# A selective-scan stage with a third buffer for its decay factors, and its gate moved behind the recurrence

## What is computed

```python
xz = x @ in_proj_w.T
u, res = jnp.split(xz, 2, axis=-1)
...
u = jax.nn.silu(conv)
delta = jax.nn.softplus(dt @ dt_proj_w.T + dt_proj_b)
A = -jnp.exp(A_log)
def step(h, t):
    delta_t, B_t, C_t, u_t = t
    dA = jnp.exp(delta_t[..., None] * A)
    h = dA * h + delta_t[..., None] * B_t[:, None, :] * u_t[..., None]
    y = jnp.einsum('bdn,bn->bd', h, C_t)
    return (h, y)
...
y = jnp.swapaxes(ys, 0, 1) + u * D_skip
y = y * jax.nn.silu(res)
return y @ out_proj_w.T
```

## Time and profile before

| | |
|---|---|
| median of three runs | 7221.53 us (7217.19 to 7222.52) |
| profiled execution, its own time | 7217.93 us |
| its span, first to last instruction | 7216.2 us |
| mean granted TensorE clock | 0.875 of full speed |
| DMA | 1297.78 MB |

### The profile page before, as it was taken

How to read it: one execution, slowest core, us unless ns; L and a number is a source line. 1 busy time by engine, 2 the same in 40 slices (tenths; PEclk the granted TensorE clock), 3 DMA queues, 4 the chain that set the end, 5 groups by cost and what they waited for, 6 DMA issues and landing times. The chain is left out here.

```text
span 7216.2 us, 70913 instructions
## 1 busy us (share of the span) xinstructions
PE 5483.0 (76%) x16640; PEld 2999.0 (42%) x16640; DVE 5886.2 (82%) x7907; ACT 3552.3 (49%) x5338; POOL 4301.8 (60%) x2865
## 2 busy tenths in 40 slices
PE   4788778888887888878788888888887888599700
PEld 1344444444444444444444444444444444466400
DVE  5999999999999999989999999999999998211255
ACT  3555555555555555555555555555555554111156
POOL 3666666666666666666666666666666666200176
PEclk8899898889999988898988889989989988699855
DMA  7656556655655555555555555555555555022253
GB/s 262 215 193 197 192 198 200 202 195 195 203 203 188 194 194 191 195 189 194 193 190 189 193 191 200 193 192 189 196 194 184 187 188 194 11 91 87 78 160 94
DMA packets 492087, 1297.78 MB, mean 180 GB/s; under 512 B 59311, under 2 KB 216625, under 8 KB 490561
## 3 DMA queue, kind: packets, MB, share of 16 engines
q1 hardware_dynamic: 440960, 1219.82, 50.7%
q10 hardware_dynamic: 26048, 38.95, 1.6%
q0 software_dynamic: 24576, 33.72, 1.5%
HBM read 1206.19 MB, written 119.54 MB: 184 GB/s over the span
## 5 line engine op out<-in xcount | busy, mean ns | idle before, releaser
L480 POOL TENSOR_TENSOR st<-st,C_rows 128x1024 f32<-128x1024 f32 x1024 | 2470.6, 2415 | 1155.7 <-DVE st L988 1154.3
L787 PE MATMUL y<-st,ident 128*128 128x512 f32 x4096 | 2163.0, 663 | 472.2 <-POOL st L480 426.5
L988 DVE TENSOR_TENSOR_SCAN st<-dA,drive 128x1024 f32<-128x1024 f32 x1024 | 2338.7, 2284 | 177.2 <-ACT dA L642 85.2
L642 ACT ACTIVATE dA<-delta,a_neg 128x511 f32<-128x511 f32 x2048 | 1382.3, 713 | 2155.2 <-DVE st L988 2146.7
L787 PEld LDWEIGHTS y<-st,ident 128*128 128x128 f32 x4096 | 830.3, 212 | 1520.0 <-issue 899.1
L960 DVE TENSOR_TENSOR drive<-du,B_rows 128x1024 f32<-128x1024 f32 x1024 | 1259.5, 1230 | 101.3 <-DVE du L955 18.2
L761 PE MATMUL pre_bank<-e_abs,in_w 128*128 128x512 f32 x1024 | 601.6, 718 | 178.2 <-DVE u L926 161.9
L1388 POOL DMA_INDIRECT rows<-expert_out,idx_c x256 | 266.3, 1040 | 621.5 <-DVE idx_c L1435 551.4
L555 POOL DMA_INDIRECT expert_in<-tb,idx x256 | 259.8, 1015 | 367.0 <-DVE idx_all L1163 306.0
L741 PE MATMUL post_bank<-d_w,gT 128*128 128x256 f32 x2048 | 467.0, 385 | 12.4 <-issue 11.6
L741 PEld LDWEIGHTS post_bank<-d_w,gT 128*128 128x128 f32 x2048 | 394.3, 193 | 119.9 <-issue 67.7
(11 more groups left out here) (190 smaller groups left out, 8027.8 us busy)
## 6 DMA issues: line engine op xcount, KB each, us to landing
B_rows<-bc_rows SPq DMA_DIRECT2D x1024, 512.0 KB
C_rows<-bc_rows SPq DMA_DIRECT2D x1024, 512.0 KB
xin<-in_x SPq DMA_DIRECT2D x32, 512.0 KB, 7.3
expert_in<-gT ACTq DMA_DIRECT2D x8, 2048.0 KB, 27.2
xn_rows<-xin SPq DMA_DIRECT2D x32, 512.0 KB, 6.2
h<-xn_rows SPq DMA_DIRECT2D x32, 512.0 KB, 6.5
x_res<-in_x SPq DMA_DIRECT2D x32, 512.0 KB, 3.6
x_rows<-x_res SPq DMA_DIRECT2D x32, 512.0 KB, 3.2
```

Of the source, the lines that this page charges most:

```text
L480: pool.tensor_tensor(tile[:, :, :], tile[:, :, :], bc[1][k % ROWS[1]][:, :, :], ALU.mult)\
L642: return act.activation(dA[k % 2][:, j, 1:L], delta[par][:, c, 1:L], ACT.Exp, scale=a_neg[:, c, n:n + 1])
L787: last = pe.matmul(Y[:, :], ident[:, :], st[k % RING][:, j, :], start=pair == 0 and j == 0, stop=pair == CU - 1 and j == 1)
L988: dve.tensor_tensor_scan(st[k % RING][:, :, :].rearrange("p a l -> p (a l)"), dA[k % 2][:, :, :].rearrange("p a l -> p (a l)"), DR[:, :, : ...
```

## The change

`dA` gets a third buffer (`AHEAD = 3`), and ScalarE fills `dA` two units ahead of the recurrence in place of one. Units 0 and 1 of a sequence are made at the end of the one before. On VectorE the gate of a finished chunk is called at the end of `recur`, in slot 3k+1, and slot 3k is empty. The counts of `consts` rise by one, for the third buffer's memset.

```diff
+    AHEAD = 3
...
-        dA = [sb(f"dA{i}", [P, 2, L]) for i in range(2)]
+        dA = [sb(f"dA{i}", [P, 2, L]) for i in range(AHEAD)]
...
                 yield 95
-                decay(b, par, 0, 0)
-                decay(b, par, 0, 1).then_inc(scan_exp.did(0), 1)
+                for k in range(AHEAD - 1):
+                    decay(b, par, k, 0)
+                    decay(b, par, k, 1).then_inc(scan_exp.did(k), 1)
...
-                    act.wait_ge(*(scan_h.at(NU - 2 + k, b - 1) if k < 2 else scan_h.at(k - 2, b)))
-                return act.activation(dA[k % 2][:, j, 1:L], delta[par][:, c, 1:L], ACT.Exp,
+                    act.wait_ge(*(scan_h.at((NU - 1 - k) // AHEAD * AHEAD + k, b - 1) if k < AHEAD
+                                  else scan_h.at(k - AHEAD, b)))
+                return act.activation(dA[k % AHEAD][:, j, 1:L], delta[par][:, c, 1:L], ACT.Exp,
                                       scale=a_neg[:, c, n:n + 1])
...
                 def first_half(k):
-                    if k + 1 < NU:
-                        decay(b, par, k + 1, 0)
+                    if k + AHEAD - 1 < NU:
+                        decay(b, par, k + AHEAD - 1, 0)
...
                 def recur(k):
-
                     dve.wait_ge(*scan_exp.at(k, b))
                     dve.wait_ge(*scan_in.at(k, b))
                     dve.wait_ge(*(scan_sum.at(NU - RING + k, b - 1) if k < RING else scan_sum.at(k - RING, b)))
                     dve.tensor_tensor_scan(st[k % RING][:, :, :].rearrange("p a l -> p (a l)"),
-                                           dA[k % 2][:, :, :].rearrange("p a l -> p (a l)"),
+                                           dA[k % AHEAD][:, :, :].rearrange("p a l -> p (a l)"),
                                            DR[:, :, :].rearrange("p a l -> p (a l)"), 0.0,
                                            ALU.mult, ALU.add).then_inc(scan_h.did(k), 1)
-                run_slots(stages, (chunk_done, recur, ahead))
+                    chunk_done(k)
+                run_slots(stages, (nothing, recur, ahead))
```

More of the change, by code:

```diff
@@ L118, in attention_phase @@
     KD, KI, KF, NX, CAP, NSLOT, FAR = (env[k] for k in ("KD", "KI", "KF", "NX", "CAP", "NSLOT", "FAR"))
-    CU, NU, RING, ROWS = (env[k] for k in ("CU", "NU", "RING", "ROWS"))
+    CU, NU, RING, AHEAD, ROWS = (env[k] for k in ("CU", "NU", "RING", "AHEAD", "ROWS"))
     x_v, xn_v, x1_v, xe_dram, bc_dram, xe_zero_v = (
@@ L426, in _ @@
             pool.memset(minus_half[:, :], -0.5).then_inc(consts, 1)
-            for i in range(2):
+            for i in range(AHEAD):
                 pool.memset(dA[i][:, :, 0:1], 0.0).then_inc(consts, 1)
@@ L432, in _ @@
                       allow_small_or_imprecise_dtypes=True).then_inc(consts, 1)
-            pool.wait_ge(consts, 11)
+            pool.wait_ge(consts, 12)
             pool.affine_select(out=ident[:, :], in_=ident[:, :], compare_op=ALU.not_equal, fill=1.0, base=0,
@@ L571, in _ @@
                 act.dma_start(xe_zero_v[a], gT_flat).then_inc(zeroed, 16)
-            act.wait_ge(consts, 13)
+            act.wait_ge(consts, 14)
             act.wait_ge(pre_weights_in, 16 * len(PRE_IN))
@@ L646, in first_half @@
                 def first_half(k):
-                    if k + 1 < NU:
-                        decay(b, par, k + 1, 0)
+                    if k + AHEAD - 1 < NU:
+                        decay(b, par, k + AHEAD - 1, 0)
                 def second_half(k):
-                    if k + 1 < NU:
-                        decay(b, par, k + 1, 1).then_inc(scan_exp.did(k + 1), 1)
+                    if k + AHEAD - 1 < NU:
+                        decay(b, par, k + AHEAD - 1, 1).then_inc(scan_exp.did(k + AHEAD - 1), 1)
                 run_slots(stages, (first_half, second_half, nothing))
@@ L725, in _ @@
                 steps.credit(pe)
-            pe.wait_ge(consts, 13)
+            pe.wait_ge(consts, 14)
             pe.wait_ge(pre_weights_in, 16 * len(PRE_IN))
@@ L898, in _ @@
                 steps.credit(dve)
-            dve.wait_ge(consts, 13)
+            dve.wait_ge(consts, 14)
             dve.wait_ge(pre_weights_in, 16 * len(PRE_IN))
```

## The result

The changed kernel takes 7274.45 us (7269.44 to 7283.53, four runs) against 7221.15 (7217.19 to 7222.52, four runs) for the kernel before in the same comparison: a ratio of 1.0076, 95% interval 1.0059 to 1.0094. It is slower, the direction that had the largest chance, and 4.45 us beyond the upper end of the range. The profiled execution spans 7267.7 us, 51.5 more than before. The lines moved by 1 to 3: L988 is now L990, L787 L790, L741 L744, L1085 L1088, L937 L940, L960 L963, L966 and L969 are L969 and L972, L642 is L645.

A forecast was written before the change was run, and what follows sets the result against it. VectorE (busy 82%) and TensorE (76%) were taken as nearly full. Per sequence −0.7 + 0 + 0.15 + 1.55 = +1.0 us, times 30, less 8 and 4, gave +18: 7235.9 us, with 3.6 for the median 7240; range 7185 to 7270.

The forecast's parts named there:

- Wait at unit 22: VectorE's 1.19 us wait for `dA` goes, L937 then waits 0.4 to 0.5 us: gain 0.7 us a sequence.
- Gate at unit 18: VectorE's mean 1.5 us wait goes, but a longer L937 at unit 20 pays it back: gain 0.
- Gate at unit 10: The gate's 0.55 us wait goes, but VectorE then waits 0.7 us for POOL's `x_res`: loss 0.15 us.
- Gate at unit 26: The gate, which had no wait, comes later: TensorE 2.4 us later, its idle time from 1.03 to 3.4 us.
- Wait at unit 29: The 1.49 us `dA` wait goes, but unit 31's recurrence waits for the ring buffer: all lost again.
- TensorE's clock: Behind unit 26's gap the clock falls, three chances in four; TensorE 3.8 us late, mean loss 1.55 us a sequence.
- The second rival: TensorE keeps its clock behind the gap at unit 26: −0.4 us a sequence, 7197 us; 22%.
- the first number: Unit 31's recurrence starts 1.4 us later; taken as the loss at sequence ends where the loop goes back.
- The sum: +1.0 us in each of 30 sequences, less 8 for slow stretches and 4 for other `dA` waits: +18 us.
- (1): Rival: the `dA` and gate waits just vanish, 4.7 us in each of 30 sequences, 7080 us; 6%.

The follow-up runs named there:

- e1: The changed kernel with all gates in front of the recurrence again, so the third buffer alone: 7122.51 us, 0.9902 of the kernel before.
- e3: The changed kernel with only the gate at unit 26 back in front of the recurrence: 7124.48 us, 0.9900 of the kernel before.
- e4: The changed kernel with four matmuls of the MLP's first product issued twice, in front of TensorE's gap: 7213.59 us, 1.0024 of the kernel before.
- e9: The changed kernel with the edits of e4 and e5 together: 7170.1 us, 0.9964 of the kernel before.
- e5: The changed kernel with SyncE's row loads held, at a loop pass's first unit, until VectorE has done unit 0: 7244.84 us, 1.0011 of the kernel before.
- e7: The changed kernel with four sequences to a pass of the hardware loop, not two: 7249.71 us, 1.0017 of the kernel before.

## Why the prediction was wrong, step by step

**Wait at unit 22** gains: the wait is gone and L940 takes 0.87 us and not 0.68, so 0.2 of it is lost and not the 0.4 to 0.5 of the text; in e1 units 21 to 23 take 0.91 us less, for 0.7.

**Gate at unit 18**: right. L940 grew to 8.21 us here, and from L1164 (before L1161) to its end it is 32.55 us in nearly all sequences, as before. A wait in front of a long wait is worth nothing. The Trainium skill's page SBUF — State Buffer, section "SBUF: two separate sides", says that VectorE and GpSimd share a port; the 8.21 us of an instruction that takes 0.68 elsewhere, ended with POOL's series, agree, and show more: this instruction gets no turn between two of POOL's products.

**Gate at unit 10**: right, L909 waits 0.70 us for `x_res`, and unit 15 comes 0.13 us later than before (0.15 forecast). e3 confirms that both gates together are worth nothing.

**Gate at unit 26**: right, TensorE waits 3.40 us.

**Wait at unit 29**: right, the 1.49 us came back as a wait for the ring buffer, 1.70 us even with a fast clock (e4); 1.5 was forecast. With a slow clock unit 29, which the text left out, also waits some 0.5 us for its buffer.

**TensorE's clock**: right in kind. The forecast had the fall in three sequences of four; it came in 20 of 29. From L1088 to unit 31 the changed kernel is 0.62 us slower, for the −0.7 + 0.15 + 1.4 = 0.85 of the steps ahead of the sequence's end. e4 shows its price, 0.52% with the extra matmuls paid. The second rival (the clock stays up, 7197) had its condition tried in e4, and is wrong there too: 1.0024 and not below 1. Once the loads are moved as well (e9) the ratio is 0.9964, and the rival's 7197 would be 0.9967.

**The step that failed** is in the paragraph on the clock: "At every second end of a sequence the hardware loop goes back and VectorE's own chain is the later one, so the first number counts". It let TensorE pass the branch late at no cost to what follows. Measured, the stretch behind the branch grew by 3.70 us, 13 times, 48 us. Unit 31 now waits for TensorE, and SyncE's row loads leave sooner in relation to the branch of the other two: TensorE's first L744 behind it came 4.9 us behind unit 0's start and not 2.15, as a mean, and, once it had stood so long, its matmuls ran slowly (9.49 us for 7.18). e5 moved the loads alone and the stretch fell to 28.91 us; e7 took seven of the branches away and it was gone at those. With this loss removed and the slow clock kept, e5 has 1.0011, where the sum's +18 us would be 1.0025: the rest of the sum held to some 10 us. At ends without a branch the sum had 0.3 us more for the addition of unit 31; the trace shows 0.02. I had costed the change's lateness to other engines' queues, but not when SyncE's transfers leave in relation to the branch.

**The sum** also booked −8 us for slow stretches in five sequences, which should have ended with TensorE's idle time. They didn't: in the changed kernel unit 5 waits 1.08 us behind every branch. This sits in the 3.70 us.

**The rivals.** (1), that the waits just vanish, gave 7080 for both halves together. The gates' share (0.55 and 1.5 us) never comes, in front or behind. What keeps the `dA` share away is the gate at unit 26: with that one in front (e3) the kernel gains 1%, 75 us by e1's medians, and 30 × (0.9 + 1.49) = 72 us is what the two `dA` waits alone are worth. So its mechanism holds for the buffer, and not for the gates. I had not asked what each half of the change does alone; the rows for it were there.

What stays open: e5 and the packets of q8 show that the row loads delay TensorE's fetch, but not why a packet that comes 2.5 to 3.0 us before its instructions has to wait for them. The Trainium skill's page Runtime: NRT & Kernel Launch, section "Instruction fetch mechanics", says that engines fetch their instructions by DMA and that a taken branch whose target isn't loaded yet forces a fetch, for which execution stands. This fits that the wait grew at branches alone (e7). That q8 is TensorE's queue is my inference from the constant distance. Open too is why the clock stayed up behind 9 of the 29 gaps of 3.40 us.

## What to carry to other kernels

A step that waits for nothing can be the only one that must not move: before moving a block behind another, look at who waits for it, on every occurrence, and move the occurrences separately. When a change has two halves, price each alone; here one half was worth −1.0% and hid in the other's +1.4%. When work on one engine slips around a loop's branch, look at which bulk transfers then leave at the branch; and if TensorE's clock falls in a gap that can't be closed, repeating matmuls in it may pay.

## What the runs showed of the hardware

Two loads of 512 KB, issued some 1.9 and 1.4 us before unit 0 behind a loop's branch, go with 2.8 to 4.7 us of idle time on TensorE in front of L744 (54.3 us over 13 branches); issued 2.5 us after the start of unit 0, with 1.65 to 2.3 us (24.3 over 13, e5).

Four extra matmuls a sequence, of no use, made the kernel faster by 0.5%, since a gap of 3.40 us (2.8 in one sequence) was followed by a few matmuls of 0.85 us and not 0.43 in 20 of 29 sequences, and one of 1.1 to 1.7 us never (e4).
